# Scan layers with the features on partitions: delta and C copied over lanes by DMA, u filled by 32-lane diagonals, the skip term on ACT and added to y by DVE

## The reference

```python
def layer(x, W_proj, b_proj, A_log, D, dt_bias, W_out, b_out):   # x: group-normalised
    seq = x.reshape(B, C, L).transpose(0, 2, 1)                   # L = 1024, C = 192
    proj = seq @ W_proj.T + b_proj
    x_in, delta = proj[..., :192], proj[..., 192:384]
    Bm, Cm = proj[..., 384:400], proj[..., 400:]                  # 16 states
    A = -exp(A_log)                                               # [192, 16]
    delta = softplus(delta + dt_bias)
    # for every feature d and state n, over t:
    #   h[d, n] = exp(delta[t, d] * A[d, n]) * h[d, n] + delta[t, d] * x_in[t, d] * Bm[t, n]
    #   y[t, d] = sum_n h[d, n] * Cm[t, n]
    y = y + x_in * D
    return (y @ W_out.T + b_out) back as images
```

## Time and profile before

| | before |
|---|---|
| median of 3 runs | 4769.89 us (4765.65 to 4773.83) |
| profiled execution | 4767.13 us, its span 4765.3 us |
| PE / DVE / ACT / POOL busy in the span | 87% / 69% / 50% / 49% |
| granted PE clock, mean | 0.953 |
| two scan layers | from 1721 us to the end |
| one batch of a scan layer, from store to store | about 91 us |

### The profile page before, as it was taken

One profiled execution on the slowest core, in us unless ns is written; L12 is line 12 of the kernel. 1 busy time (PEld: TensorE's weight loads), 2 busy tenths in 40 slices (PEclk: granted clock), 3 DMA queues, 4 the chain that ended last, 5 costly groups with the idle time before them and its releaser, 6 DMA issues. The chain is left out here.

```text
span 4765.3 us, 125264 instructions
## 1 busy us (share of the span) xinstructions
PE 4152.2 (87%) x51696; PEld 2707.2 (57%) x51696; DVE 3305.8 (69%) x3785; ACT 2361.6 (50%) x3289; POOL 2334.6 (49%) x749
## 2 busy tenths in 40 slices
PE   5994899999999848998998999994999999999997
PEld 5993666666666535555555555553555555555554
DVE  6554767575767527787787778782787778778776
ACT  2322343444444426656655655652655655655654
POOL 1111121212121106776676776682676676676777
PEclk9997999999999969999999999996999999999999
DMA  9524233333333210010010010011010010011011
GB/s 101 80 41 107 86 95 90 90 95 93 92 92 93 70 37 8 22 42 22 22 41 22 22 41 22 21 28 37 8 41 22 21 41 22 21 31 32 21 28 28
DMA packets 133331, 230.13 MB, mean 48 GB/s; under 512 B 14858, under 2 KB 67086, under 8 KB 132770
## 3 DMA queue, kind: packets, MB, share of 16 engines
q1 hardware_dynamic: 132804, 222.25, 19.4%
HBM read 133.14 MB, written 89.07 MB: 47 GB/s over the span
## 5 line engine op out<-in xcount | busy, mean ns | idle before, releaser
L1120 POOL TENSOR_TENSOR l_h<-l_h,l_c_rep 128x2048 f32<-128x2048 f32 x384 | 1742.8, 4544 | 707.9 <-DVE l_h L1028 700.4
L1028 DVE TENSOR_TENSOR_SCAN l_h<-l_decay,l_u_ps 128x512 f32<-128x512 f32 x768 | 891.7, 1203 | 488.8 <-PE l_u_ps L687 478.6
L687 PE MATMUL l_u_ps<-l_b_diag,l_dx_t 64*64 64x128 f32 x24576 | 857.4, 280 | 178.4 <-DVE l_h L1028 163.3
L1028 DVE TENSOR_TENSOR_SCAN l_h<-l_decay,l_h,l_u_ps 128x512 f32<-128x512 f32 x768 | 935.7, 1259 | 102.7 <-PE l_u_ps L687 102.7
L839 ACT ACTIVATE l_decay<-l_delta_rep,l_a_neg 128x1024 f32<-128x1024 f32 x768 | 848.8, 1145 | 306.1 <-DVE l_h L1028 304.0
L687 PEld LDWEIGHTS l_u_ps<-l_b_diag,l_dx_t 64*64 64x64 f32 x24576 | 688.9, 136 | 471.9 <-issue 469.0
L710 PE MATMUL l_y_ps<-l_h,l_state_sum 128*64 128x512 f32 x3072 | 773.9, 626 | 9.5 <-POOL l_h L1120 9.5
L1644 ACT ACTIVATE l_probs<-l_work 128x532 f32<-128x532 f32 (+1 forms) x384 | 217.6, 567 | 560.2 <-PE l_work L1498 553.5
L855 ACT ACTIVATE l_c_rep<-l_scratch 128x512 f32<-128x512 f32 x512 | 276.9, 593 | 381.0 <-PE l_scratch L752 380.6
L710 PEld LDWEIGHTS l_y_ps<-l_h,l_state_sum 128*64 128x64 f32 x3072 | 201.3, 141 | 356.4 <-issue 343.3
L1813 DVE RECIPROCAL l_den<-l_den 96x1024 f32<-96x1024 f32 x32 | 209.6, 6549 | 196.7 <-ACT l_den L1657 196.7
(11 more groups left out here) (170 smaller groups left out, 6487.2 us busy)
## 6 DMA issues: line engine op xcount, KB each, us to landing
l_x<-x_after_l SPq DMA_DIRECT2D x48, 768.0 KB, 7.8
l_x_res<-x_after_l SPq DMA_DIRECT2D x48, 768.0 KB, 5.6
l_qk_parts<-l_qk SPq DMA_DIRECT2D x48, 768.0 KB, 4.8
x_after_l<-l_x_res SPq DMA_DIRECT2D x32, 768.0 KB, 5.0
l_x<-x SPq DMA_DIRECT2D x64, 192.0 KB, 8.8
x_after_l<-l_x SPq DMA_DIRECT2D x64, 192.0 KB, 4.1
out<-l_x_res SPq DMA_DIRECT2D x16, 768.0 KB, 4.3
l_q_a<-l_qk_parts SPq DMA_DIRECT2D x32, 256.0 KB, 3.2
```

Of the source, the lines that this page charges most:

```text
L687: made = nc.tensor.matmul(u_ps[64 * par:64 * par + 64, 2 * win + r, 128 * c:128 * c + 128], dx_t[rows, n.s, 4 * win + c, 64 * db:64 * db + ...
L1028: nc.vector.tensor_tensor_scan(h[:, s % S_RING, npi, t], decay[:, 2 * (s % 2) + npi, t], u, start, ALU.mult, ALU.add).then_inc(scanned, 1)
L1120: nc.gpsimd.tensor_tensor(view, view, c_rep[:, 2 * q:2 * q + 2, :], ALU.mult).then_inc(c_applied, 1)
```

## The change

Only the scan layers change. Projections are made with the features on partitions and time along them (`de`, `x`, `bc`; 512 moving columns, the two column halves of the array for the two halves of time `g`). delta (`take_delta`) is softened in that layout; DMAs copy it over the lanes into `delta_rep` (SBUF to SBUF), four per feature block. C goes by DMA to DRAM and comes back repeated over 64 partitions into `c_rep`, two DMAs per quarter. `dx` is made by DVE in the feature layout and turned by PE (`turn_dx`), copied by ACT (`take_dx`); B is turned too (`turn_b`). The diagonals hold 32 lanes and not 64, so `fill_u` has 32 matmuls per window with 32 rows and 64 moving columns. The skip term is ACT's copy of the x projection, scaled by D, into `y_sb`, and DVE adds `y_ps` to it (`keep_y`). Slots, the place of soft_log, finish_delta and add_residual, and SP's list change with it.

```diff
@@ fill_order
-        "a0": ["c2.0", "c2.1"], "b0": ["c2.2", "c2.3", "rep2.0", "rep2.1"],
-        "a1": ["norm", "c3.0", "c3.1"], "b1": ["c3.2", "c3.3"],
-        "a2": ["tail.0", "tail.1"], "b2": ["tail.2", "tail.3"],
-        "a3": ["sp.0", "sp.1"], "b3": ["sp.2", "sp.3"],
-        "b5": ["xbc.0", "xbc.1"], "b6": ["xbc.2"], "a7": ["xbc.3"],
-        "b8": ["rep0.0", "rep0.1"], "a9": ["rep1.0", "rep1.1", "cf.0", "cf.1"],
-        "a10": ["c0.0", "c0.1"], "b10": ["c0.2", "c0.3"],
-        "a11": ["c1.0", "c1.1"], "b11": ["c1.2", "c1.3"],
+        "a1": ["norm"], "a2": ["tail.0", "tail.1"],
+        "a3": ["de.0"], "b3": ["de.1"], "a4": ["de.2"], "b4": ["tail.2", "tail.3"],
+        "a5": ["bc"], "a6": ["x.0"], "b6": ["x.1"], "a7": ["x.2"],
+        "b7": ["dx.0", "dx.1"], "b8": ["dx.2"],
...
@@ sync, main (m = after(n))
+                    load_c(n, 3)
...
+                            sp.wait_ge(xn_made, m.count(1, 1))
+                            load(after(m))
+                        store_c(m)
+                        sp.wait_ge(delta_made, m.count(1, 1))
+                        load_delta(m, 0)
+                        load_delta(m, 1)
                     if not n.first:
                         store(before(n))
                         sp.wait_ge(out_stored, n.count(16, 0))
+                        load_residual(n)
+                    if not is_last(n):
+                        sp.wait_ge(c_stored, m.count(32, 32))
+                        sp.sem_inc(c_store_seen, 1)
+                        load_c(m, 0)
+                        load_c(m, 1)
+                        sp.wait_ge(decay_made, m.count(TILES_S, 0))
+                        load_delta(m, 2)
+                        load_c(m, 2)
@@ sync, helpers
+                def load_c(n, q):
+                    if not n.first:
+                        sp.wait_ge(c_applied, n.count(S_STEPS, q - 3))
+                    for par in range(2):
+                        rows = c_dram[n.s].rearrange("(q i a) t -> q a i t", i=2, a=2)[q, par]
+                        sp.dma_start(c_rep[64 * par:64 * par + 64, 2 * q:2 * q + 2, :],
+                                     rows[None, :, :].to_broadcast([64, 2, L])).then_inc(c_loaded[q], 16)
+                def load_delta(n, db):
+                    for g in range(2):
+                        for par in range(2):
+                            sp.dma_start(delta_rep[64 * par:64 * par + 64, db, :].rearrange("p (a g z) -> p g a z", a=4, g=2)[:, g],
+                                         delta[64 * g:64 * g + 64, db, :].rearrange("p (a z) -> p a z", a=4)).then_inc(rep_loaded[db], 16)
@@ tensor, fill_u
-                    for c in range(4):
-                        for r in range(2):
-                            rows = slice(64 * r, 64 * r + 64)
+                    for c in range(8):
+                        k, g = divmod(c, 2)
+                        for r in (2 * win, 2 * win + 1):
+                            rows = slice(32 * r, 32 * r + 32)
                             for par in range(2):
-                                made = nc.tensor.matmul(u_ps[64 * par:64 * par + 64, 2 * win + r, 128 * c:128 * c + 128],
-                                                        dx_t[rows, n.s, 4 * win + c, 64 * db:64 * db + 64],
-                                                        b_diag[rows, npq, 4 * win + c, par, :], start=True, stop=True)
+                                at = 256 * g + 64 * k
+                                made = nc.tensor.matmul(u_ps[64 * par:64 * par + 64, r, at:at + 64],
+                                                        dx_t[rows, n.s, db, k, 64 * g:64 * g + 64],
+                                                        b_diag[rows, npq, c, par, :], start=True, stop=True)
@@ tensor
+                def project(n, f, wt, db):
...
+                    for ci in range(2):
+                        for g in range(2):
+                            last = nc.tensor.matmul(scratch[64 * g:64 * g + 64, f.bank, :], wt[:, ci, 64 * db:64 * db + 64],
+                                                    xn[:, n.s, ci, g, :], start=(ci == 0), stop=(ci == 1))
+                def turn_dx(n, f, db):
+                    await_drained(pe, fill(n, f"x.{db}"))
+                    for k in range(4):
+                        last = nc.tensor.transpose(scratch[:, f.bank, 128 * k:128 * k + 128], dx[:, db, 128 * k:128 * k + 128],
+                                                   ident[:, :])
@@ tensor, main
                         make_slot(n, f"b{s}")
+                        if s == 7 and not is_last(n):
+                            turn_b(after(n))
@@ scalar
+                def skip_term(n, db):
+                    f = fill(n, f"x.{db}")
+                    await_fill(act, f)
+                    nc.scalar.activation(in_order(y_sb[:, n.s, db, :]), by_lane(scratch[:, f.bank, :]), ACT.Copy,
+                                         scale=d_skip[:, db:db + 1]).then_inc(skip_made, 1)
...
-                        if s == 4 and not last:
+                        take_slot(n, f"a{s}")
+                        if s == 6 and not last:
                             soft_log(after(n))
-                        take_slot(n, f"a{s}")
@@ vector
+                def make_dx(n, db):
+                    f = fill(n, f"x.{db}")
+                    if db == 0:
                         dve.wait_ge(delta_made, n.count(1, 1))
+                    dve.wait_ge(skip_made, n.count(3, db + 1))
...
+                def keep_y(n, db):
+                    dve.wait_ge(y_summed, n.count(S_STEPS, 4 * db + 4))
+                    nc.vector.tensor_tensor(y_sb[:, n.s, db, :], y_ps[:, :], y_sb[:, n.s, db, :], ALU.add).then_inc(y_kept, 1)
...
+                            if s == 7:
+                                make_dx(after(n), 0)
...
                         scan(n, s, 1, 0)
                         scan(n, s, 1, 1)
+                        if s == 1 and not n.first:
+                            keep_y(before(n), 2)
+                        if s in (5, 9):
+                            keep_y(n, s // 4 - 1)
...
+                            if s in (7, 8):
+                                make_dx(after(n), s - 6)
@@ gpsimd, main
-                        if s in (2, 6) and not n.first:
-                            add_residual(before(n), s // 4)
-                        if s == 4 and not last:
+                        if s in (3, 6) and not n.first:
+                            add_residual(before(n), s // 6)
+                        if s == 5 and not last:
                             finish_delta(after(n))
```

More of the change, by code:

```diff
@@ L674, in fill_u @@
                     db, npq = divmod(s, 4)
-                    if s == 0 and win == 0:
-                        for j in (2, 3):
-                            await_drained(pe, fill(n, f"xbc.{j}"))
+                    if npq == 0 and win == 0:
+                        await_drained(pe, fill(n, f"dx.{db}"))
                     if db == 0 and win == 0:
@@ L693, in skip @@
-                def skip(n, db):
-                    if not (n.first and db == 0):
-                        pe.wait_ge(y_kept, n.count(3, db))
-                    for ci in range(2):
-                        for win in range(2):
-                            nc.tensor.matmul(y_ps[64 * win:64 * win + 64, :], w_skip[:, ci, 64 * db:64 * db + 64],
-                                             by_chunk[:, n.s, ci, win].rearrange("p c r j -> p r c j"),
-                                             start=(ci == 0), stop=False)
+                                at = 256 * g + 64 * k
@@ L731, in replicate_delta @@
-                def replicate_delta(n, f, db, i):
-                    pe.wait_ge(delta_made, n.count(1, 1))
-                    for k in range(4):
-                        for par in range(2):
-                            last = nc.tensor.matmul(scratch[64 * par:64 * par + 64, f.bank, 128 * k:128 * k + 128],
-                                                    delta_t[:, 4 * i + k, 64 * db:64 * db + 64], ident[:, :],
-                                                    start=True, stop=True)
-                    last.then_inc(filled, 1)
@@ new lines, in project, with project_bc @@
+                    last.then_inc(filled, 1)
+                def project_bc(n, f):
+                    pe.wait_ge(xn_made, n.count(1, 1))
+                    for ci in range(2):
+                        for i in range(4):
+                            which, g = divmod(i, 2)
+                            last = nc.tensor.matmul(scratch[32 * i:32 * i + 32, f.bank, :], w_bc[:, ci, 32 * which:32 * which + 32],
+                                                    xn[:, n.s, ci, g, :], start=(ci == 0), stop=(ci == 1))
+                    last.then_inc(filled, 1)
@@ L755, in project_out @@
                 def project_out(n, co):
-                    fs = [fill(n, f"tail.{2 * co + win}") for win in range(2)]
+                    fs = [fill(n, f"tail.{2 * co + g}") for g in range(2)]
```

(18 more changed lines are left out.)

374 lines of the change are left out of this document (161 added, 213 removed).

## The result

| | before | after |
|---|---|---|
| median | 4767.77 us (4 runs) | 4913.02 us (4 runs, 4898.84 to 4934.38) |
| ratio | | 1.0309, 95% interval 1.0267 to 1.0351 |
| profiled execution | 4767.13 us | 4898.84 us |

A forecast was written before the change was run, and what follows sets the result against it. PE was nearly always at work; each step was priced at the larger of PE and DVE. Batch 90.2 to 87.5 us, times 32, gives -86, edges -14: 4667 us profiled, 4670 median; range 4500 to 4870.

The forecast's parts named there:

- PE's work: PE in the scan layers: about 14 us less work a batch, with a u fill at 1.06 us against 1.03.
- rival 2: A u fill is paid per instruction: 1.75 us gives 4950 us (8%), 2.1 us gives about 5200 (5%).
- The table and the walk: Twelve steps at the larger of PE and DVE: 89.5 to 80.7 us; walked through with waits, batch 87.0.
- (a): Step 3: PE's first `de` waits for ACT's normalised xn, ready at 26.5 against 24.1; 2.4 us lost.
- (b): Steps 6 to 8 become serial through ACT's logarithm, POOL's delta, make_dx and dx turns; about 4 us a batch.
- (c): Low clock after PE's idle stretches of 2 to 4 us in steps 9 to 0; 0.5 us added a batch.
- Two signs that the prediction named: Granted clock under 0.95 would speak for Rival 3; a batch under 84 or over 90 us makes the forecast wrong.
- Rival 3: PE goes cold three or four times a batch, 1.7 us lost each in steps 2 to 8: 4750 to 4800; 18%.
- DMA: SP's copies of C, delta and x total 83 us serially inside the 87.5 us batch, so nothing on the path.
- rival 4: C or delta lands late, or a wait blocks SP's queue: 5 us a batch, 4830 us; 7%.
- Edges: Each layer's first scan comes 7 us earlier, 14 for two layers, between 0 and 20.

The follow-up runs named there:

- e13_no_c_rest: Changed kernel with logarithm and normalise one step earlier and PE's program written out, C's copies cut to 1 KB from each layer's second batch: 4489.44 us, ratio 0.9415.
- e5_no_c: Changed kernel with C's 512 KB copies cut to 1 KB from each layer's second batch on (C is stale): 4736.03 us, ratio 0.9926.
- e12_norm_alone: Changed kernel with only ACT's normalise moved from step 3 to step 2: 4736.03 us, ratio 0.9935.
- e3_soft_early: Changed kernel with ACT's logarithm passes in step 5 instead of 6, and SP waiting before delta's second block is overwritten: 4733.50 us, ratio 0.9933.
- e6_no_c_soft: e3_soft_early with C's 512 KB copies cut to 1 KB from each layer's second batch on: 4642.03 us, ratio 0.9731.
- the three pairs: With and without C's copies: changed kernel and e5_no_c; e3_soft_early and e6_no_c_soft; the 4549.82 us version (logarithm, normalise early, PE written out) and e13_no_c_rest.
- e1_warm: Changed kernel with 25 pairs of zero matmuls a batch placed where PE waits: 5009.49 us, ratio 1.0517.

## Why the prediction was wrong, point by point

- **PE's work.** Right. A fill of u at full clock lasts 1.16 us as the timeline models it, 64 matmuls, against 1.10; from start to next start it is 1.09 (2075.42 to 2076.51) where the forecast took 1.06 against 1.03, and rival 2, the cost per instruction, did not come. The rule of about 25 ns between starts ("TensorE: Matmul & The Clock Gate", Back-to-back issue gap, in the Trainium skill) would have made it 1.6 us by the prediction's estimate; the trace disagrees. Projections on 64 output rows last 1.94 us, as long as the state sums of the earlier trace rows, which is what was said of them. PE is not busy near 72 us a batch as forecast, but 83.5, as in before: 30.4 us of the batch are at half speed. With less of that (11.6 us), in e13_no_c_rest, it is 74.9.
- **The table and the walk.** Right for a batch without low clock and issue waits: 87.0 us was said, and 87.0 is the sum of the fastest cases. The walk holds in its places too: it had the scans of step 9 start 27.4 us after PE's start of step 5, and in the fastest batches they start after 27.5.
- **(a), the wait for xn.** Right in place and length: 74.2 us in 30 waits, 2.3 in each inner batch; 2.4 was said.
- **(b), the serial path.** Right in its first half: DVE waits 244.3 us in 32 for delta (25 of it is one wait, so 7.1 each; 15.9 less 9.1, or 6.8, was said), and undoing it takes 4.7 us from steps 6 and 7, where about 4 was said. PE's own wait in it, for dx, is 76.9 us in 32.
- **(c), the clock: the step that failed.** "DVE leads there, so I add only 0.5" looked for low clock in steps 9 to 0. But (a) and (b) themselves make PE idle, for 2.3 us in front of step 4 and 2.2 us in step 7, longer than the 1.80 us that low clock followed in before, and the sum gives nothing for what follows them. Low clock is 30.4 us a batch and not 3.8. In step 4, where PE leads, it cost 2.9 us a batch over (a), nearly six times the 0.5 of the forecast; it lasted up to 10.24 us in a place, and not 3.4. Step 8 has 5.4 us of it and is 1.0 over its fastest case. Two signs that the prediction named came: a granted clock under 0.95 (0.874) and a batch over 90 us. Rival 3 had the mechanism, with three or four places of 3.4 us and 1.7 us for each; its 4750 to 4800 was too low by its size and by the next point.
- **DMA: the second step that failed.** "So nothing on the path" failed, in a way that no rival named. No copy came late for its reader, which is what rival 4 was about. Yet the copies of C cost 177 us by e5_no_c, as PE stopped for "issue" while they ran, part of it by way of low clock; that it waits for its instructions is the likely reading. A copy of C also took 6.8 us to land (median) where 3.7 was put in the sum, and one of delta 2.5 where it was 3.
- **Edges.** The first scan came 15.9 us earlier (1775.9 where it was 1791.8); 7 was said for a layer. From the start of the last batch of the first layer to the second's first scan it is 150.1 us where it was 166.4, but that stretch holds the last batch too.

The sum, by the starts of the scans: the 30 batches that another one follows took 167 us more than in before, where 81 less was forecast (30 of 2.7). All the rest (the way to the first scan, the border with the first layer's last batch, the last batch to the end) took 36 less, where 19 less was forecast. 248 too much and 16 too little make the 232 by which the profiled execution missed its forecast.

How the 9.2 us split: e12_norm_alone takes 2.9 from step 4 beyond (a). e5_no_c takes 5.2 from the batch, of which 1.5 is in the same step 4, so the two overlap and can't be added. What the overlap consists of stays open: without the copies, step 4 is in low clock for 3.0 us and not 6.3, though the wait for xn is as long (74.2 us in 30, both). The second pair of runs doesn't repeat it: from e3_soft_early to e6_no_c_soft step 4 stays at 13.1 and 12.8 us, its low clock at 6.6 and 6.1. So the price of the copies depends on what stands beside them: 177, 91 and 60 us in the three pairs. I have no run that tells why.

## What to carry to other kernels

Price an ordering wait on PE by what comes after it: where PE sets the pace behind the wait, add half of the low-clock time that follows, and look for the cheapest move that lets the producer finish a step earlier. And when a change moves work from PE to DMA, look in the timeline for bursts that stop in the middle with "issue" behind them, and take the copies out in one run to see what they cost: the profile counts the queue of instructions among the same 16 DMA engines. Whether more instructions in a burst make it worse was not tried alone.

## What the hardware showed that was not expected

- PE's fill of u stopped in mid-burst 62 times, for 0.2 to 3.9 us (75 issue waits with those at a fill's start, the longest 5.6 us), with DMA engines 77% busy during the waits. In the kernel before, with 640 fewer matmul records a batch and copies in other steps, engines 90% busy for 23.6 us of a batch left 4.8 us of such waits in the whole run.
- The same wait of 2.3 us on PE was followed by none, 3.4, 6.8 or 10.2 us of low clock, in a step that is otherwise the same from batch to batch.
- Zeros that PE multiplied in its waits brought the mean clock to 0.953 in e1_warm, from 0.874, and made the kernel 96 us slower.
- 32x64 matmuls in float32 with their own loads, spread by the program over four parts of the array: 64 in 1.16 us, 18 ns each.
